# Attention scores and weighted values as full 128-wide products in a graph layer on one Trainium2 core

## What is computed

```
ea  = edge_attr @ w_e                          # 131072 x 256
agg = segment_sum(relu(x[src] + ea), dst)      # 8192 x 256, dst is sorted
h_local = bn1(relu((x + agg) @ w1) @ w2 + x)
q, k, v = split(x.reshape(256, 32, 256) @ in_w.T)      # 256 graphs of 32 nodes, 4 heads of 64
attn = softmax(q k^T / 8)                              # per graph and head, 32 x 32
h_attn = bn2((attn v) @ out_w.T + x)
out = h_local + h_attn
out = bn3(out + relu(out @ m_w1) @ m_w2)
x = layernorm(x + out)
```

## Time and profile before

| | |
|---|---|
| median of 3 runs | 1954.65 us (1941.84 to 1976.45) |
| the profiled execution | 1932.73 us, its span 1930.9 us |
| mean granted TensorE clock in it | 0.865 of full speed |
| busy share TensorE / VectorE / ScalarE / GpSimd | 81% / 39% / 42% / 50% |
| TensorE records | 11522 products, as many weight loads |

### The profile page before, as it was taken

One profiled execution on the slowest core, in us unless ns is written; L12 is line 12 of the kernel. 1 busy time (PEld: TensorE's weight loads), 2 busy tenths in 40 slices (PEclk: granted clock), 3 DMA queues, 4 the chain that ended last, 5 costly groups with the idle time before them and its releaser, 6 DMA issues.

```text
span 1930.9 us, 30540 instructions
## 1 busy us (share of the span) xinstructions
PE 1567.5 (81%) x11522; PEld 1182.9 (61%) x11522; DVE 761.7 (39%) x1465; ACT 817.6 (42%) x1729; POOL 970.3 (50%) x1032
## 2 busy tenths in 40 slices
PE   5878888887878888887777887888888787888787
PEld 3556566565656666665666665666666566666566
DVE  4334433343333433433433443433433333433343
ACT  2334434453334444444444443444444444444452
POOL 6554534555445555554455554645555455555430
PEclk6779888898888988888888887989888888888899
DMA  8545533444333434433443433433433334433321
GB/s 292 166 164 178 183 109 99 118 125 121 96 93 113 131 116 118 122 111 93 118 120 110 123 105 104 133 113 113 125 104 114 111 117 114 121 106 107 108 86 34
DMA packets 107385, 233.42 MB, mean 121 GB/s; under 512 B 21731, under 2 KB 46563, under 8 KB 105189
## 3 DMA queue, kind: packets, MB, share of 16 engines
q0 software_dynamic: 49152, 134.28, 24.1%
q1 hardware_dynamic: 56640, 93.87, 14.9%
q10 hardware_dynamic: 1444, 3.30, 0.5%
HBM read 206.20 MB, written 25.17 MB: 120 GB/s over the span
## 4 chain that ended last, share of the span: by engine, by line
PE 66%; issue 15%; another core or an unknown queue 9%; ACT 4%; DVE 4%; DMA 0%; POOL 0%; DVEq 0%; ACTq 0%
PE bank L670 26%; PE bank L716 15%; PE bank L698 14%; PE bank L800 5%; PE bank L786 2%; DVE ml L527 2%; ACT mh L316 2%; PE bank L870 1%; PE bank L704 1%; ACT bank L310 1%; PE bank L725 1%; PE bank L809 1%; ACT h L327 0%; DVE onehot L543 0%
## 5 line engine op out<-in xcount | busy, mean ns | idle before, releaser
L280 POOL DMA_INDIRECT xg<-xb_dram,srcs x864 | 817.2, 946 | 755.5 <-ACT bank L310 520.0
L527 DVE SCALAR_TENSOR_TENSOR ml<-bank,mh 128x512 fp32r<-128x512 f32 x512 | 349.2, 688 | 963.3 <-ACT mh L316 781.4
L316 ACT ACTIVATE mh<-bank 128x512 fp32r<-128x512 f32 x512 | 300.4, 601 | 978.1 <-PE bank L698 551.7
L716 PE MATMUL bank<-mh,onehot 128*128 128x256 f32 x1024 | 346.9, 358 | 123.1 <-DVE ml L527 103.7
L716 PEld LDWEIGHTS bank<-mh,onehot 128*128 128x128 f32 x1024 | 210.7, 206 | 264.5 <-issue 221.6
L310 ACT COPY bank<-xg 128x512 f32<-128x512 f32 x512 | 307.5, 601 | 69.8 <-DVE ml L527 32.8
L698 PE MATMUL bank<-we,ea 64*128 64x256 f32 x2048 | 334.9, 449 | 0.5 <-issue 0.5
L716 PE MATMUL bank<-ml,onehot 128*128 128x256 f32 x1024 | 288.8, 301 | 0.0
L698 PEld LDWEIGHTS bank<-we,ea 64*128 64x128 f32 x2048 | 200.7, 211 | 99.8 <-issue 71.4
L280 POOL DMA_INDIRECT xg<-in_x_dram,srcs x160 | 152.1, 950 | 143.9 <-ACT bank L310 98.8
L716 PEld LDWEIGHTS bank<-ml,onehot 128*128 128x128 f32 x1024 | 215.3, 210 | 1.6
(11 more groups left out here) (100 smaller groups left out, 1319.5 us busy)
## 6 DMA issues: line engine op xcount, KB each, us to landing
ea<-in_ea_dram SPq DMA_DIRECT2D x128, 256.0 KB
xg<-xb_dram,srcs POOLq DMA_INDIRECT x864
xT<-in_xT_dram SPq DMA_DIRECT2D x32, 256.0 KB
aggT<-in_xT_dram SPq DMA_DIRECT2D x32, 256.0 KB
xrow<-in_x_dram SPq DMA_DIRECT2D x8, 1024.0 KB
xb_dram<-xrow SPq DMA_DIRECT2D x8, 1024.0 KB
oT_dram<-oT SPq DMA_DIRECT2D x32, 256.0 KB
xn<-in_x_dram SPq DMA_DIRECT2D x32, 256.0 KB
```

Of the source, the lines that this page charges most:

```text
L280: pool.indirect_dma_start(xg[:, q % NX, n * C:(n + 1) * C], None, t["x"] if q < XB_PAIR else k.xb_dram[:, :], bass.IndirectOffsetOnAxis(k. ...
L316: nc.scalar.activation(mh[:, q % 4, :], EA[q % 3][:, :], ACT.Relu).then_inc(s_mh, 1)
L527: nc.vector.scalar_tensor_tensor(ml[:, q % 4, :], EA[q % 3][:, :], 0.0, mh[:, q % 4, :].bitcast(fp32), ALU.max, ALU.subtract).then_inc(s_m ...
L716: ins = nc.tensor.matmul(G[n % 2][:, 0:C], onehot[:, n % 2, 2 * j + two, :], half[:, q % 4, two * C:(two + 1) * C], start=j == 0 and two = ...
```

## The change

Scores become one product per head and half block: all 128 nodes against all 128 nodes, contraction 64, 128x128 results, 8 products instead of 32. Three quarters of each result, the blocks of one graph against another, are never read. The two score banks `X[0]` and `X[2]` are now the halves of one two-bank tile `both`, so that one access can span all eight heads and half blocks. The blocks on the diagonal lie at different columns in each quarter of 32 partitions, so VectorE's maximum, subtraction and transpose are each four instructions over 32 partitions (8 x 32 elements) instead of two, two and one over 128.

`probT` is now [128, 8, 128] with the transposed probabilities on the block diagonal and zeros elsewhere, which one memset sets at the start. With it the weighted values are 8 products (contraction 128, `vn` stationary with 64 columns, `probT` moving with 128), and their results already have channels on partitions: two heads fill the upper and lower 64 partitions of `X[1]`. So the copy to `on`, the four transposes and their semaphores go, and ScalarE's copy to `oT` stands at p = 14 of the same block.

```diff
-        k.bank = [... f"bank{n}", [P, 512], fp32)) for n in range(8)]
-        k.EA, k.G, k.X = k.bank[0:3], k.bank[3:5], k.bank[5:8]
+        k.bank = [... f"bank{n}", [P, 512], fp32)) for n in range(6)]
+        k.EA, k.G = k.bank[0:3], k.bank[3:5]
+        k.both = ctx.enter_context(nc.psum_tensor("both", [P, 1024], fp32))
+        k.X = [k.both[:, 0:512], k.bank[5], k.both[:, 512:1024]]
...
-        k.prob, k.probT = sb("prob", [P, 2 * H, NPG]), sb("probT", [P, 2 * H, NPG])
+        k.prob, k.probT = sb("prob", [P, 2 * H, NPG]), sb("probT", [P, 2 * H, P])
-        k.on = sb("on", [P, 2 * C])
...
 scalar, attention
                 if p == 14:
                     act.wait_ge(s_av, i + 1)
-                    if i >= 1:
-                        act.wait_ge(s_oT, i)
-                    nc.scalar.copy(k.on[:, :], X[1][:, :]).then_inc(s_on, 1)
-                if p == PI:
-                    act.wait_ge(s_oT, i + 1)
                     if i >= 2:
                         act.wait_ge(s_p2, i - 1)
...
 vector
+            step_of(nc.vector.memset(k.probT[:, :, :], 0.0))
...
+                quarter = [slice(n * NPG, (n + 1) * NPG) for n in range(P // NPG)]
+                scores = k.both[:, :].rearrange("p (h n) -> p h n", n=P)
                 if p == 9:
                     dve.wait_ge(s_sc, i + 1)
-                    for n in range(2):
-                        ins = nc.vector.tensor_reduce(k.mx[:, H * n:H * n + H], scores[n],
-                                                      AX.X, ALU.max)
+                    for g in quarter:
+                        ins = nc.vector.tensor_reduce(k.mx[g, :], scores[g, :, g], AX.X, ALU.max)
...
+                    for g in quarter:
                         ins = nc.vector.tensor_tensor(
+                            k.dif[g, :, :], scores[g, :, g],
+                            k.mx[g, :].unsqueeze(2).to_broadcast([NPG, 2 * H, NPG]), ALU.subtract)
...
-                    nc.vector.transpose(k.probT[:, :, :].rearrange("p h n -> p (h n)"),
-                                        k.prob[:, :, :].rearrange("p h n -> p (h n)")
-                                        ).then_inc(s_prob, 1)
+                    for g in quarter:
+                        ins = nc.vector.transpose(k.probT[g, :, g], k.prob[g, :, :])
+                    ins.then_inc(s_prob, 1)
...
 tensor, scores
-                            col = (2 * b + c) * NPG
-                            for n in range(4):
-                                o = b * P + n * NPG
-                                ins = nc.tensor.matmul(
-                                    X[2 * (h % 2)][n * NPG:(n + 1) * NPG, col:col + NPG],
-                                    k.qT[at:at + DH, c, o:o + NPG], k.kT[at:at + DH, c, o:o + NPG],
-                                    start=True, stop=True)
+                            col = (2 * b + c) * P
+                            ins = nc.tensor.matmul(X[2 * (h % 2)][:, col:col + P],
+                                                   k.qT[at:at + DH, c, row], k.kT[at:at + DH, c, row],
+                                                   start=True, stop=True)
...
 tensor, weighted values
-                            for n in range(4):
-                                r = slice(n * NPG, (n + 1) * NPG)
-                                ins = nc.tensor.matmul(
-                                    X[1][r, b * C + h * DH:b * C + (h + 1) * DH],
-                                    k.probT[r, H * (h % 2) + 2 * b + h // 2, :],
-                                    k.vn[r, b, h * DH:(h + 1) * DH], start=True, stop=True)
+                            at, col = DH * (h % 2), h // 2 * NB + b * P
+                            ins = nc.tensor.matmul(X[1][at:at + DH, col:col + P],
+                                                   k.vn[:, b, h * DH:(h + 1) * DH],
+                                                   k.probT[:, H * (h % 2) + 2 * b + h // 2, :],
+                                                   start=True, stop=True)
...
-                if p == 15:
-                    pe.wait_ge(s_on, i + 1)
-                    for c in range(CC):
-                        for b in range(2):
-                            ins = nc.tensor.transpose(
-                                X[1][:, c * NB + b * P:c * NB + (b + 1) * P],
-                                k.on[:, b * C + c * P:b * C + (c + 1) * P], ident[:, :])
-                    ins.then_inc(s_oT, 1)
```

16 lines of the change are left out of this document (3 added, 13 removed).

## The result

| | before | changed |
|---|---|---|
| median | 1950.05 us (4 runs, 1941.84 to 1976.45) | 1824.71 us (4 runs, 1817.45 to 1834.31) |
| ratio | 1 | **0.937**, 95% interval 0.931 to 0.944 |
| span of the profiled execution | 1930.9 us | 1823.4 us |
| granted TensorE clock, mean | 0.865 | 0.894 |
| TensorE busy / idle in the span | 1567.5 / 363.4 us | 1467.2 / 356.2 us |

The change made the kernel 6.3% faster; forecast were 3.8% and 1880 us, with a range of 1730 to 1975. **The numbers hold for this chip only.** The experiments ran on whichever chip was free, and the kernel before takes one of two kinds of time: 1950 us here and 1892 on one chip of the experiments ("stalling"), 1361 to 1363 on three others ("quiet").

What follows compares the result with a forecast made beforehand. TensorE was taken as the bound, stalling ahead of scores and values during gathers. Per block 1.6 + 0.8 + 0.5 - 0.6 = 2.3 us, 74 us over 32 blocks, gave 1859 in the profile, scaled to 1880 us; range 1730 to 1975.

Steps and rivals of the forecast that it cites:

- partial relief: Central outcome for the whole kernel: part of the stall goes, 1830 to 1925 us, chance 0.40.
- a stall that goes by half or more: Outcome in which TensorE's stall falls by half or more: 1680 to 1830 us, chance 0.24.
- The rate of the stalled stretch: TensorE during runs of gathers: it advances by instructions, not columns, at 0.18 us per instruction.
- The two stages: Scores and weighted values on TensorE: 4.6 to 3.8 and 7.0 to 5.4 us per block, saving 0.8 and 1.6.
- upper bound: New scores or values stage in a stalled stretch: at most 32 x 0.18 = 5.7 us each.
- lower bound of 1.8: New scores or values stage at full rate: 16 records at 0.11 us, 1.8 us each.
- the charge of 0.6 us a block for VectorE: VectorE's maximum, subtraction and transpose: 3.5 us added per block, about 3 of it hidden, 0.6 charged.
- Rival two: Stall lasts as long as the gathers and holds up whatever is next: 1922 to 1955 us, no change, chance 0.19.
- Rival four: VectorE's attention chain becomes what TensorE waits for: +3.0 us a block, +96 us, about 2050 us, chance 0.11.
- Rival three: Slower by the array where no gathers run: +1.3 us a block, +42 us, 1997 us, chance 0.06.
- The tiling rule: Skill page on TensorE: products of 32 run in up to 16 tiles at once; filling the array with zeros wastes that.
- Rival one: Small instructions are the whole stall: 7.9 us a block saved, about 1700 us; its branch, half or more, 0.24.

Runs made afterwards that it cites:

- the second chip: The unmodified changed kernel run again on a stalling chip of the experiments, against the kernel before at 1892.14 us there: 1836.05 us, ratio 0.966.
- the kernel without gathers: Changed kernel with GpSimd's gathers only for the first eight pairs, on a quiet chip: 1434.12 us, ratio 1.052 to the kernel before with its gathers.
- the early v product: Changed kernel with the v product moved from slots 10 and 11 to slot 4, on a stalling chip: 1886.36 us, ratio 0.999 to the kernel before.
- the split products: Changed kernel with each score and values product cut into four of 32 moving columns, on a quiet chip: 1594.28 us, ratio 1.169 to the kernel before.
- the kernel with one instruction each on VectorE: Changed kernel with maximum, subtraction and transpose as one 128-partition instruction each: 1353.42 us, ratio 0.993 to the kernel before; 1355.91 us, 0.995 on a second quiet chip.

## Why the prediction came out as it did

The time lay in the range and the sign was right. The median of 1824.71 us lies just below the branch called partial relief (1830 to 1925), in the one that had 0.24 for a stall that goes by half or more; the stall's cost per block fell only from 17.8 to 14.1 us. By TensorE's records, the size of 3.8% against 6.3% is the difference of two terms that were both far too small; that the time is still near is partly luck, as the two errors have opposite signs.

**The rate of the stalled stretch** (0.18 us per instruction while gathers run) held, on wide products too, in the rows at 947.73 to 950.61. That stall ends follow the last gather by 1.7 us held as well: 1.8 at 950.09. That the stall is there because of the gathers was an argument from their coincidence and has remained one: no experiment without gathers met a stalling chip, and three quiet chips run the same gathers at no cost.

**The two stages: mis-sized.** The values were put at 5.4 us, near the upper bound of 32 x 0.18, the scores at 3.8, midway between the bounds. By their records both came out at 1.0 to 1.16 us with no idle time of the product engine ahead of them, below my lower bound of 1.8. The lower bound failed because 0.11 us per record was borrowed from 128-column transposes; the product records follow each other at 0.07. The upper bound failed for the records although the row against it was in my hands: in the earlier trace rows 27 records with their loads, 54 instructions, stand at full pace inside the stalled stretch before the steps begin (in the kernel before, at least 18 records of every values stage, on either stalling chip, stand ahead of its first step of over 0.9 us). The records of a stage of 32 instructions fit into such a start; no run with another size tested it. Stages and transposes fell from 393.1 to 72.2 us, 10.0 us a block, where 2.9 were forecast.

The results do not come so early. From first record to semaphore the new stages take 6.3 + 4.0 = 10.3 us a block here and 3.8 + 5.4 = 9.2 on the second chip, and the forecast for them was 3.8 + 5.4 = 9.2. So in sum the price of the stages in the stall was about right, though not how it splits between the two here. What the working had wrong is where it shows: it counted the stages by records alone, and a stage whose records pass early makes its readers wait instead.

**What is paid back: mis-sized.** By the records, the charge of 0.6 us a block for VectorE, with nothing for a stall that moves, was 6.7 us in fact, (320.9 - 107.5) / 32. The v product, busy and idle together, grew from 69.3 to 238.8 us, 5.3 us a block, and `mh`'s `sum_pair` line from 470.0 to 532.2, 1.9 a block; all other lines together took 0.6 less. Part of this is the late semaphores of the stages themselves; how much, no run on a stalling chip separates from VectorE's added work, which alone makes the v product wait 1.8 us a block (57.0 / 32) in the kernel without gathers. The length of VectorE's added work was right: its steps are 419, 420 and 436 ns on 32 partitions against the 409, 409 and 445 taken from rows of 128.

```profile
L586 DVE STREAM_TRANSPOSE probT<-prob 32x256 f32<-32x256 f32 x128 | 55.8, 436 | 2.4
...
L568 DVE TENSOR_TENSOR dif<-both,mx 32x256 f32<-32x256 f32 x128 | 53.7, 420 | 2.4
L564 DVE TENSOR_REDUCE mx<-both 32x8 f32<-32x256 f32 x128 | 53.7, 419 | 64.5 <-remote 63.2
```

The Trainium skill, VectorE: DVE Perf Modes, section Why `tensor_reduce` can't reduce along partition axis, calls each of the 128 partition lanes an independent pipeline along the free dimension; these rows agree, a quarter of the partitions costs the same. What failed is the cover. I set the 2.2 us added there against VectorE's own idle time behind the subtraction, but the v product doesn't wait behind that idle time: it waits for `dif` itself. It was already next in TensorE's order, with little or nothing between, so every bit of delay to `dif` counts at once. Idle time behind an instruction covers the instructions that follow on its engine, never a reader of the instruction itself. The waits of the changed kernel (us in total, times, longest) say so, and below them one block in order of time:

```profile
PE both L664 <- DVE dif L568: 115.9, 26, 5.8
...
DVE mx L564 <- remote: 63.2, 20, 4.1
ACT ex L350 <- DVE dif L568: 62.5, 24, 2.7
```

```profile
981.52 1.16 PE L779 MATMUL both<-kT,qT 64*128 64x128 f32 x16
...
990.17 1.72 DVE L564 TENSOR_REDUCE mx<-both 32x8 f32<-32x256 f32 x4 [3.35 <-remote]
...
991.93 1.72 DVE L568 TENSOR_TENSOR dif<-both,mx 32x256 f32<-32x256 f32 x4
...
993.71 2.07 PE L664 MATMUL both<-iwT,xT 128*128 128x256 f32 x4 [4.74 <-DVE dif L568]
```

Here both costs add up: the scores' semaphore rises only at 990.15, 7.5 us after their last record and behind a run of gathers that ends at 988.8, and then VectorE's eight instructions take 3.5 us before TensorE may go on. The four records behind take 2.07 us where the same four take 1.13 or 1.03 on a quiet chip. The granted clock fell during the 4.74 us of idle and is 0.50, the lower of its two levels, all through these four records. That is a cost which the prediction's sum had left out. The first four v records run at this level in 24 of 32 blocks on this chip, in 8 of 32 on the second, and in none behind the first three blocks of the kernel before, where they take 1.03 us. Over the whole run the clock was no loss, its mean rose from 0.865 to 0.894.

**Rival two, the stall only moves** (0.19), describes the idle time best, though not as a constant: 363.4 to 356.2 on the first chip, 340.3 to 362.2 on the second, and in the early v product 395.5. It gave no change in time because it reckoned the busy time of the old stages as part of the stall that stays; that part is what was won.

**Rival four, VectorE** (0.11), was right in its mechanism everywhere, and in its sign on quiet chips: 3.0 us a block forecast, 2.1 measured by the period (41.8 against 39.7). On the stalling chips its price is paid out of a larger saving.

**Rival three, the array** (0.06): 1.3 us a block forecast. Quiet chips give +0.4 for the scores (1.16 against 0.76), nothing for the values (1.09 against 1.10) and -0.6 for the transposes: about nothing in sum, as the kernel with one instruction each on VectorE says too (0.993 and 0.995). The tiling rule that stood behind it is right, as the split products show, but eight full products instead of 32 packed ones just about break even.

**Rival one, all stall gone** (0.24): no; idle time and issue gaps stayed.

**The signs.** That stall ends follow the gathers and that idle time ahead of `ml` shrinks (963.3 to 777.5 us) held. That line 791's stage takes some 5 us where gathers run failed for its records, 1.1 us in every block, and is near for its semaphore, 4.0 and 5.4 us. Rival two's and rival four's signs came as well: more idle time ahead of line 710 (123.1 to 184.9 us), and the v product waiting for `dif`.

## What to carry to other kernels

Where a wait for "issue" stands ahead of small products, ask first what a machine without that wait does: here one program took 1362 us on three chips and 1892 and 1950 where it stalled, and the change that gains 3.4 to 6.3% on the one kind loses about 5% on the other (without gathers). Don't take a stage's records for its end: here they passed in 1.2 us and the semaphore came up to 7.5 us later, so look at when its readers go on. When a stall coincides with something that runs beside the engine, expect its idle time to move to the next work. The busy time that is removed is no sure gain either: 100.3 us of it went with 107.5 us of span on the first chip, 89.7 with 67.8 on the second, and 81.0 with 25.8 in the early v product. Before an added instruction is called hidden, list the readers of its result, not the idle time behind it on its own engine: for eight instructions in place of four, the reader on another engine paid 1.7 us in nearly every block of a quiet chip. The half of the change that leaves the scores alone is the version to keep on quiet chips, for less than 1% (0.991 and 0.992, the shortest time there of all kernels that compute the whole layer).

## What was not expected of the hardware

- Two kinds of chips, or of their state at the time, for one program: TensorE busy in 81 to 82% of 1907 to 1931 us on stalling ones, 97% of 1349 to 1356 us for kernels close to it on quiet ones, with gathers of the same length (0.95 us) on both. What differs between them is open.
- In the stalled stretches read, products with 32, 64 and 256 moving columns alike advance at 0.18 us per instruction.
- A product's record can end long before its semaphore rises: the scores whose records stand at 981.52 to 982.68 signalled at 990.15 and were read at 990.17. In kernels on quiet chips the scores' semaphore came at most 0.6 us behind.
- Score records of 32 and of 128 moving columns follow each other at the same 0.07 us; those that go round the quarters of the array at 0.012.
- 1008 gathers on GpSimd cost a quiet chip 3 us of 1361.
